# A decoder layer on one core: five kinds of PE step parted by their inputs, and a new written order

## What is computed

```python
x = x + self_attention(layernorm(x))            # 16 heads, rotary, T = 256
x = x + cross_attention(layernorm(x), ctx)      # 16 heads, 77 keys
h = layernorm(x); nodes = {-1: h}
for c in range(6):                              # FFN stage: 8 heads, T = 256
    q = ew[c, 0] * (nodes[c - 1] @ We[eq] + be[eq])
    k = ew[c, 1] * (nodes[snode] @ We[ek] + be[ek])
    v = ew[c, 2] * (nodes[mid] @ We[ev] + be[ev])
    o = mha(q, k, v, Wq[c], Wk[c], Wv[c], Wo[c])
    nodes[c] = act_w[c] * o + q
x = x + layernorm(nodes[5]) * ln_g + ln_b
```

## Time and profile before

| | |
|---|---|
| median of three runs | 5605.14 us (5601.58 to 5607.79) |
| the profiled execution | 5609.61 us, its span 5607.0 us |
| PE busy | 5142.0 us, 92% of the span |
| DVE, ACT, POOL busy | 51%, 45%, 12% |
| mean granted TensorE clock | 0.945 |
| DMA | 8 GB/s on average |
| one round in the middle | 337.9 us |

### The profile page before, as it was taken

The page is one execution under the profiler, slowest core; times in us unless marked ns, Lnnn a source line. Parts: engine busy times, 40 slices in busy tenths (PEclk is TensorE's granted clock), DMA queues, the critical chain, the costliest instruction groups (busy, mean ns, idle before and its releaser), DMA issues.

```text
span 5607.0 us, 154314 instructions
## 1 busy us (share of the span) xinstructions
PE 5142.0 (92%) x64216; PEld 3781.3 (67%) x64216; DVE 2855.0 (51%) x5090; ACT 2527.1 (45%) x4784; POOL 655.8 (12%) x1753
## 2 busy tenths in 40 slices
...
GB/s 120 6 2 10 3 2 11 2 11 2 7 5 2 11 2 10 3 2 11 2 11 2 6 7 2 11 2 10 3 2 11 2 10 3 6 7 2 11 2 7
DMA packets 45078, 46.66 MB, mean 8 GB/s; under 512 B 11968, under 2 KB 44096, under 8 KB 44352
## 3 DMA queue, kind: packets, MB, share of 16 engines
...
## 4 chain that ended last, share of the span: by engine, by line
issue 82%; POOL 9%; PE 2%; DVE 2%; POOLq 1%; DVEq 0%; ACT 0%; ACTq 0%
POOL neg_max L649 3%; POOL neg_max L652 2%; PE banks L856 2%; POOL x_tok L634 2%; POOL inv_std L628 1%; POOL rope_c L641 1%; DVE n_tok L788 0%; DVE rope_s L801 0%; POOL var_eps L625 0%; POOL node_t L659 0%; POOL node_t L656 0%; POOLq L648 0%; POOLq L651 0%; PE banks L915 0%; DVE rope_s L797 0%
## 5 line engine op out<-in xcount | busy, mean ns | idle before, releaser
L826 DVE TENSOR_REDUCE row_max<-banks 128x4 f32<-128x1024 f32 (+1 forms) x1288 | 1317.6, 1069 | 746.6 <-PE banks L856 711.3
L740 ACT ACTIVATE probs<-banks 128x1024 f32<-128x1024 f32 (+1 forms) x1288 | 1147.3, 936 | 608.0 <-PE banks L856 604.1
L856 PE MATMUL banks<-q_parts,k_parts 32*128 32x256 f32 x12384 | 591.6, 302 | 114.1 <-DVE row_max L826 69.4
L856 PEld LDWEIGHTS banks<-q_parts,k_parts 32*128 32x128 f32 x12384 | 464.3, 192 | 308.9 <-DVE row_max L826 187.4
L856 PE MATMUL banks<-k_parts,q_parts 32*128 32x256 f32 x12432 | 527.5, 302 | 148.2 <-DVE row_max L826 68.6
L837 DVE TENSOR_TENSOR probs<-banks,context_t 128x256 f32<-128x256 f32 x449 | 190.0, 423 | 903.2 <-ACT context_t L752 899.7
L856 PE MATMUL banks<-node_t,w_n 128*128 128x256 f32 x2560 | 641.7, 386 | 0.4
L856 PEld LDWEIGHTS banks<-k_parts,q_parts 32*128 32x128 f32 x12432 | 430.0, 193 | 298.9 <-issue 133.1
L649 POOL TENSOR_TENSOR neg_max<-row_max,zeros 128x8 fp32r<-128x8 f32 x644 | 141.5, 220 | 3749.5 <-DVE row_max L826 3749.5
L856 PEld LDWEIGHTS banks<-node_t,w_n 128*128 128x128 f32 x2560 | 461.9, 190 | 93.8 <-issue 26.3
L750 ACT ACTIVATE context_t<-banks 128x256 f32<-128x256 f32 x514 | 196.6, 383 | 611.6 <-PE banks L856 607.4
...
## 6 DMA issues: line engine op xcount, KB each, us to landing
...
```

The costliest lines, as they stand in the source:

```text
L740: done(act.activation(probs[s][0:rows, g % 2, 2 * p:2 * p + 2, 0:kt, :] .rearrange("p c k t -> p c (k t)"), psum[0:rows, b0:b0 + 2, 0:kt * T],
L826: done(dve.reduce_max(row_max[s][:, g, 2 * p:2 * p + 2, :].rearrange("p c q -> p (c q)"), psum[:, b0:b0 + 2, :].rearrange("p c (q t) -> p ...
L856: return nc.tensor.matmul(bank_ap, lhs, rhs, start=start, stop=stop, **kw)
```

## The change

The steps that wait for several inputs are parted, each part with its own wait. The number of matmuls stays 3080 in a round.

- `S` becomes `S` (16 matmuls with the high part of the queries) and `SB` (8 with the low part). `S` now waits for `QH` and `KL`, `SB` for `QL`.
- `ST` becomes `ST` (24) and `SX` (8, the maxima). `ST` now waits for `QL` and `KL`, and `SX` for `MR`. The `start` flag is given once for a bank instead of once for each half of it.
- `Q` becomes `Q` and `QB`, one input half of the features each, each waiting for its half of the node.
- `OUT` becomes, in a node, `OA` (4 matmuls on the query input) and `OB...0` and `OB...1` (2 each, by halves of the context, each waiting for its `NR`); in stages 0 and 1 only the two `OB`.
- `NE`, `QH` and `QL` of the stages behind the first are named by halves, with a semaphore step each; their instructions stay as they were.
- `ORDER` is new for all steps, with other banks, and 135 steps stand ahead of the loop instead of 109 (438 matmuls instead of 398).

```diff
 def last_scores(s, j):
-    return "ST", s, j, last_group(j)
+    return "SX", s, j, last_group(j)
...
-def shares_bank(key):
-    return key[0] == "PV" and place(*key[2:])[1] == 1
+def began(key):
+    if len(key) < 3:
+        return None
+    k, s, j = key[:3]
+    if k == "PV" and place(*key[2:])[1] == 1:
+        return "PV", s, j, key[3] - 1
+    if k in ("SB", "SX"):
+        return ("S" if k == "SB" else "ST",) + key[1:]
+    if k == "QB":
+        return "Q", s, j
+    if k == "OB" and (j >= FFN0 or key[3]):
+        return ("OA", s, j) if j >= FFN0 else ("OB", s, j, 0)
+    return None
...
-MX1.0.0.0 MX1.0.0.1 XB1.0 +LOADX0 MX1.0.1.1 MX1.0.1.0 S1.0.2@0 MX1.0.2.0 MX1.0.2.1 S1.0.3@4 MX1.0.3.1 MX1.0.3.0
+XB0.1 +LOADX0 MX1.0.2.1 SB1.0.3 MX1.0.3.0 MX1.0.3.1 S0.1.0@4 SB0.1.0 MX0.1.0.0 MX0.1.0.1 NM1.0.2 S0.1.1@0
...
-                wait_for(pe, at, a, ("low_kept", ("QL", s, j)), ("low_kept", ("KL", s, j)))
+                q_half = (s, j, 1 if j == SELF else x)
+                if k == "S":
+                    wait_for(pe, at, a, ("high_kept", ("QH",) + q_half), ("low_kept", ("KL", s, j)))
+                else:
+                    wait_for(pe, at, a, ("low_kept", ("QL",) + q_half))
...
-                    for n, (qp, kp) in enumerate(((0, 0), (0, 1), (1, 0))):
+                    for qp, kp in ((0, 0), (0, 1)) if k == "S" else ((1, 0),):
...
-                wait_for(pe, at, a, ("max_rows_kept", ("MR", s, j, x)))
+                wait_for(pe, at, a, ("low_kept", ("QL", s, j, 1 if j == SELF else x)), ("low_kept", ("KL", s, j)))
...
+            elif k == "SX":
+                x, e = place(j, a[3])
+                wait_for(pe, at, a, ("max_rows_kept", ("MR", s, j, x)))
...
-            elif k == "OUT":
-                wait_for(pe, at, a, *[("normalized", ("NR", s, j, x)) for x in range(KC)],
-                         *([node_kept(s, j, "q")] if j >= FFN0 else []))
+            elif k in ("OA", "OB"):
+                wait_for(pe, at, a, *(node_kept(s, j, "q") if k == "OA" else [("normalized", ("NR", s, j, a[3]))]))
```

More of the change, by code:

```diff
@@ L119 @@
 ORDER = """
-MX1.0.0.0 MX1.0.0.1 XB1.0 +LOADX0 MX1.0.1.1 MX1.0.1.0 S1.0.2@0 MX1.0.2.0 MX1.0.2.1 S1.0.3@4 MX1.0.3.1 MX1.0.3.0
[L121 to L128, removed]
-MX1.1.2.0 S1.1.3@4 MX1.1.3.0 MX1.1.3.1 NM1.1.3 NM1.1.2 MT1.1.0@1 MR1.1.0 ST1.1.0@4 LNS0.2 EX1.1.0.1 MT1.1.1@2
@@ L165 @@
-LNP0.7 VE1.7 +S0.0.0@0 +MX0.0.0.0 +MX0.0.0.1 +NM0.0.0 PV1.7.0@4 RC1.7.0 NR1.7.0 MR1.7.1 ST1.7.1@0 +S0.0.1@4
-+MX0.0.1.1 +MX0.0.1.0 EX1.7.1.0 EX1.7.1.1 +S0.0.2@0 +NM0.0.1 +MX0.0.2.0 +MX0.0.2.1 +S0.0.3@4 +MX0.0.3.1
-+MX0.0.3.0 +MT0.0.0@1 +MR0.0.0 PV1.7.1@3 LNN0.7 +NM0.0.2 +NM0.0.3 RC1.7.1 +ST0.0.0@4 NR1.7.1 +EX0.0.0.0
-+MT0.0.1@0 FG0 +MR0.0.1 +EX0.0.0.1 +ST0.0.1@0 FX0 STORE0 +PV0.0.0@4 OUT1.7@5 FA1 +XB0.0 +LOADX1 +LNS1.0
-+EX0.0.1.0 +EX0.0.1.1 +ST0.0.2@0 +EX0.0.2.1 +EX0.0.2.0 +PV0.0.1@4 +LNP1.0 LNS1.7 LNP1.7 LNN1.7 +ST0.0.3@0
```

304 lines of the change are left out of this document (169 added, 135 removed).

## The result

| | before | after |
|---|---|---|
| median | 5605.07 us (5601.58 to 5607.79) | 5446.78 us (5445.1 to 5450.77, 4 runs) |
| ratio | | 0.9719, 95% interval 0.9702 to 0.9736 |
| profiled span | 5607.0 us | 5449.0 us |
| PE busy | 5142.0 us | 5088.6 us |
| mean granted clock | 0.945 | 0.953 |

A forecast was written before the change was run, and what follows sets the result against it. PE, busy 92% of the span, was taken to bound the kernel. Terms -3.2 + 0.3 - 1.0 - 3.2 + 1.0 = -6.1 us per round, times 16 = -98, +3 start-up, gave 5510 us, range 5435 to 5585.

The forecast's parts named there:

- the sum without the seams: Whole round: the forecast gain before any cost for added waits between parts, 7.1 us per round.
- The likeliest case, as forecast: Whole run: the summed gains hold, 5470 to 5550 us, chance 52%.
- the first rival, the clock gains too: End and middle: less waiting shrinks low-clock stretches, half of at most 8 us per round, 5445 us; chance 15%.
- The clock: Whole round: PE busy time at full clock stays; halving it in two low-clock stretches would give at most 8 us.
- Seams: Added waits inside former runs of matmuls, some 80 in score steps: cost 1.0 us per round, bounds 0 and 2.5.
- End of the round: From the score steps of slot 0 to S1.0.0: minus 3.2 us per round, bounds 1.0 and 5.0.
- Head: Sixteen row-max reductions around the loop's jump: plus 0.3 us per round from PE's jump, bounds 0 and 1.5.
- Middle: At TR1.1: V1.1 moves behind OUT1.0 and fills the wait for the norm, minus 1.0 us, bounds 0.5 and 1.3.
- Cross-attention of slot 1: Stretch after the middle: nothing won, since MT1.1.0 and ST1.1.0 share bank 4 and ST waits for MR anyway.
- Nodes: Node stages: reordered fillers remove waits, minus 3.2 of 6.2 us per round, bounds 1 and 5; Q1.3 waits about 0.35.
- Start-up: Ahead of the loop: forty more matmuls and their reductions, plus 3 us once.
- The other rivals: End doesn't give, 5570 to 5590, 20%; seams cost, break-even 0.09 us each, 5615 to 5750, 9%; cancel within 0.2%, 4%.

The follow-up runs named there:

- out17_behind: Changed kernel with OA1.7, OB1.7.0, OB1.7.1 and FA1 put back behind PV0.0.0, as before the change: 5551.59 us, ratio 0.9902 to the kernel before.
- v_steps_back: Changed kernel with V0.1 back ahead of Q1.0, V1.1 back ahead of OB1.0.0, and other banks for these and PV0.1.0: 5609.32 us, ratio 1.0009.
- nodes_new_order_2: Parted steps in the old order, only the nodes from Q0.3 to Q0.7 in the new order, second cut with KH0.4 and KL0.4 ahead of Q0.3: 5610.25 us.
- new_order_joined: Changed kernel with its new order, but every part waits for all that the unparted step waited for: 5527.1 us, ratio 0.9865 to the kernel before.
- old_kernel_hinted: Kernel before the change plus a prefetch hint for the loop's jump on every engine: 5579.37 us, ratio 0.9951.

## Why the prediction was right, and where it was not

- **The whole.** PE's idle time was to fall by 7.1 us per round (the sum without the seams) and fell by 7.0 in the round read, 6.6 in the mean. That close an agreement is in part luck: the end and the head gave 1.7 us less than forecast, the middle, cross-attention and the nodes 1.5 more. The likeliest case, as forecast, was still 63 us too small, because two terms were missing or wrong in the same direction, the clock and the seams. The range held since its lower end had been set for the first rival, the clock gains too, and that is what happened: it had 5445 us and a chance of 15%.
- **The clock** is the step that failed: PE's busy time was to stay, and fell by 3.2 us in this round (3.9 in the mean). I counted the low stretches as given and looked at how short the matmuls in them are. `out17_behind` shows that waits at the end of the round bring low-clock time (27 to 34 us), and `v_steps_back` the same for the waits in the middle taken together. In `nodes_new_order_2` and `new_order_joined` it can be seen that those in the nodes don't: low-clock time stays at 31 us, and in the joined kernel, with 3.7 us more idle, at 28 against 27. Why a low stretch begins at one wait and not at another stays open: `old_kernel_hinted` lost 6 us of low clock per round with the same idle time.
- **Seams**: 1.0 us taken, 0 measured. The 32 matmuls of `ST0.3.0` with `SX0.3.0` take 1.22 us from 2936.68 on (rows below), as the prediction asked. What else is in the 0.07 us that served as a bound, no run shows.
- **End of the round**: 2.3 us of idle instead of 3.2. `ST0.0.1` and `TR1.0` lost their waits, `KR1.0` has 0.22 us, `S1.0.0` 1.67, the load comes 3.4 us earlier (4 were said), `PV1.7.1` waits 1.28 (1.4). Mis-sized was what remains ahead of the score steps: 0.50 + 0.55 + 0.93 us instead of the 1.2 at `S0.0.2` alone. `ST1.7.1` has 0.42, just over the 0.4 that I named.
- **Head**: 1.1 us more in this round (1.4 in the mean, nearly the upper bound), not 0.3. The jumps' place was right, the size wrong: PE's jump ends 0.70 us after DVE needs `SB1.0.3`, and DVE's own is no longer partly hidden.
- **Middle**: 1.5 us gone instead of 1.0, `TR1.1` waits for nothing. Cross-attention of slot 1 was to gain nothing and gained 0.7.
- **Nodes**: 3.5 us instead of 3.2 (6.4 to 2.9). `ST0.3.0` and `ST0.3.1` have no wait, `Q1.3` 0.35 as said:

```profile
2934.76 1.99 PE L893 MATMUL banks<-node_t,w_n 128*128 128x256 f32 x8 [0.35 <-ACT node_t L790]
2936.68 0.98 PE L893 MATMUL banks<-q_parts,k_parts 32*128 32x256 f32 x24
2937.49 0.41 PE L893 MATMUL banks<-max_rows,select 32*128 32x256 f32 x8
```

- **Start-up**: 3 us taken and 2.4 measured, by the first `S1.0.0`, which stands just ahead of the loop in both kernels (196.3 us before, 198.7 after). Not in the sum was the tail. From `S1.0.0` to the same one of the next round 10.4 us are gained, but from the last one to the end of the run only 4.9 (339.8 to 334.9 us), since the steps behind the last store run there too, and more of them stand behind it now. So 16 rounds are not 16 times the gain: 15 times 10.4, plus 4.9, less 2.4 is the 158 us.
- **The other rivals** fell: the end did give, and a seam costs nothing that can be measured, so the break-even price of 0.09 us was far.
